# Carried states laid out as diagonal blocks by GpSimd and multiplied by 8 full-size products behind x's transposes; x's high part on VectorE

## The reference

```python
gammas = 1.0 - 2.0 ** (-5.0 - jnp.arange(h))
q = (x @ W_q.T).reshape(b, t, h, dh)          # k and v the same
decay = jnp.where(diff >= 0, gammas[:, None, None] ** pow_, 0.0)
attn = jnp.einsum('bihd,bjhd->bhij', q, k) * decay[None] / scale
y = jnp.einsum('bhij,bjhd->bihd', attn, v)
mean = y.mean(axis=(1, 3), keepdims=True); var = y.var(axis=(1, 3), keepdims=True)
yn = ((y - mean) / jnp.sqrt(var + EPS)).reshape(b, t, dm) * gn_weight + gn_bias
x = x + yn @ W_o.T
...
shared = silu(xf @ sw1 + sb1) * (xf @ sw3 + sb3) @ sw2 + sb2
h = gelu(jnp.einsum('enc,ech->enh', xs, w1) + b1[:, None, :], approximate=False)
y = jnp.einsum('enh,ehc->enc', h, w2) + b2[:, None, :]
```

## Time and profile before

| | |
|---|---|
| median of 3 runs | 443.07 us (442.89 to 443.53) |
| profiled execution: its own time, its span | 443.2 us, 441.4 us |
| granted TensorE clock, mean | 0.996 |
| PE, PEld busy | 433.1 us, 391.6 us |
| DVE, ACT, POOL busy | 292.7, 216.3, 95.6 us |
| phase 1 | from the span's start to about 200 us |

### The profile page before, as it was taken

The page is one execution under the profiler, slowest core; times in us unless marked ns, Lnnn a source line. Parts: engine busy times, 40 slices in busy tenths (PEclk is TensorE's granted clock), DMA queues, the critical chain, the costliest instruction groups (busy, mean ns, idle before and its releaser), DMA issues.

```text
span 441.4 us, 14549 instructions
## 1 busy us (share of the span) xinstructions
PE 433.1 (98%) x6318; PEld 391.6 (89%) x6318; DVE 292.7 (66%) x685; ACT 216.3 (49%) x416; POOL 95.6 (22%) x73
## 2 busy tenths in 40 slices
PE   6999999999999999999999999999999999999997
PEld 4999999999999999998989988899988999888995
DVE  6777778766886878967556654757538575475433
ACT  3456656546754477445255443472524823346430
POOL 1103223522254213640621101211004020040000
PEclk8999999999999999999999999999999999999999
DMA  7443332232321131226230005000133001120011
GB/s 260 146 148 99 99 99 76 75 94 80 126 95 51 51 124 54 91 79 222 94 115 1 26 25 208 31 0 0 48 122 116 0 0 48 48 95 0 1 48 48
DMA packets 15382, 34.64 MB, mean 78 GB/s; under 512 B 2368, under 2 KB 2656, under 8 KB 14816
## 3 DMA queue, kind: packets, MB, share of 16 engines
q1 hardware_dynamic: 14896, 33.05, 22.0%
q10 hardware_dynamic: 432, 0.79, 0.5%
HBM read 25.44 MB, written 8.40 MB: 77 GB/s over the span
## 4 chain that ended last, share of the span: by engine, by line
PE 91%; ACT 3%; DVE 3%; DMA 1%; issue 1%; POOL 0%; DVEq 0%; ACTq 0%
PE bank L358 50%; PE bank L367 13%; PE bank L368 7%; PE bank L437 5%; PE bank L480 4%; PE bank L467 3%; PE bank L451 2%; PE bank L563 2%; PE bank L416 1%; PE bank L377 1%; ACT kexp L681 1%; ACT vexp L681 1%; DMA xin<-xa 1%; PE bank L498 1%; DVE pm L873 1%
## 5 line engine op out<-in xcount | busy, mean ns | idle before, releaser
L778 ACT ACTIVATE xres<-bank,r1b 128x256 f32<-128x256 f32 x64 | 26.8, 470 | 54.9 <-PE bank L368 53.6
L358 PE MATMUL bank<-x2hi,sw_hi 128*128 128x512 f32 x128 | 51.3, 400 | 0.0
L763 ACT ACTIVATE sil<-bank,s1b 128x512 f32<-128x512 f32 x32 | 22.0, 688 | 58.4 <-PE bank L358 58.3
L358 PE MATMUL bank<-x2lo,sw_hi 128*128 128x512 f32 x128 | 50.4, 394 | 0.0
L358 PE MATMUL bank<-x2hi,sw_lo 128*128 128x512 f32 x128 | 50.3, 393 | 0.0
L696 ACT ACTIVATE keo<-kT,msk 128x512 f32<-128x512 f32 x32 | 21.4, 715 | 51.9 <-DVE kT L862 51.9
L367 PE MATMUL bank<-sw_both,ghi 128*128 128x512 f32 x128 | 46.5, 396 | 0.0
L367 PE MATMUL bank<-w_both,ehi 128*128 128x512 f32 x128 | 46.4, 397 | 0.0
L1045 DVE SCALAR_TENSOR_TENSOR gf<-bank,s3b,sil 128x512 f32<-128x512 f32 x32 | 23.9, 748 | 32.4 <-PE bank L358 32.4
L873 DVE TENSOR_TENSOR pm<-bank,msk 128x512 f32<-128x512 f32 x64 | 39.5, 679 | 2.3 <-PE bank L437 2.2
L358 PE MATMUL bank<-xhi,wqkv_hi 128*128 128x256 f32 x128 | 38.6, 302 | 0.9 <-DVE xlo L857 0.7
(11 more groups left out here) (119 smaller groups left out, 1133.7 us busy)
## 6 DMA issues: line engine op xcount, KB each, us to landing
xin<-xa SPq DMA_DIRECT2D x16, 256.0 KB, 3.3
w_raw<-w SPq DMA_DIRECT2D x16, 256.0 KB, 3.3
xres<-xs SPq DMA_DIRECT2D x16, 256.0 KB, 3.4
x_scratch<-xres SPq DMA_DIRECT2D x16, 256.0 KB, 3.4
xl<-x_scratch SPq DMA_DIRECT2D x8, 512.0 KB, 5.2
xr<-x_scratch SPq DMA_DIRECT2D x4, 1024.0 KB, 4.8
out<-xr SPq DMA_DIRECT2D x7, 512.0 KB, 2.6
sw_raw<-sw SPq DMA_DIRECT2D x6, 256.0 KB, 3.7
```

The lines of the kernel that those rows point to most:

```text
L358: mm = nc.tensor.matmul(o, w[c][l], x[c][r], start=first and c == 0 and j == 0, stop=last and c == n - 1 and j == 2)
L763: nc.scalar.activation(sil[i % 2][:], h1_bank[i % 2][:], ACT.Silu, bias=s1b[:, m:m + 1]).then_inc(sil_ready, 1)
L778: ge = nc.scalar.activation(hf[q % 2][:, m, :], e_bank[q % 4][:, m * 2 * P:(m + 1) * 2 * P], ACT.Gelu, bias=r1b[:, e, m:m + 1])
```

## The change

The 32 small products of a step's from_state become 8 full-size ones (6 where s is 0): a new buffer `wide` (128 partitions x 2 groups x 4 chunks x 128 columns) holds the four 32x32 states of a group and chunk as blocks on the diagonal of a 128x128 matrix, zero elsewhere. GpSimd clears it once and copies the blocks in with four copies of 32 partitions in every step (widen_state), before its other work of the step. from_state stands between transpose_x(h+2) and scores(h+1). high_x, apart from its first two calls, is DVE's; ACT takes high_y behind copy_k and copy_v; DVE takes low_y and y_sums last. The loads of slot_bias stand behind phase 1's last stores, and its buffer has another place in SBUF.

```diff
-            def from_state(h, opens):
-
-                pe.wait_ge(s_ready, h + 1)
...
-                        for p in range(PAIRS):
-                            at = slice(32 * p, 32 * p + 32)
-                            mm = nc.tensor.matmul(y_bank[at, o:o + CH], state[h % 2][at, g, c, :], qT[h % 2][at, g, c * CH:(c + 1) * CH],
-                                                  start=(opens and c == first and g == 0), stop=not opens, skip_group_check=True)
...
+            def from_state(h):
+
+                pe.wait_ge(wide_ready, h + 1)
+                for c in range(0 if h % NSUP else 1, CPS):
                     for g in range(GROUPS):
                         o = g * SUPER + c * CH
...
+                        mm = nc.tensor.matmul(y_bank[:, o:o + CH], wide[:, g, c, :], qT[h % 2][:, g, c * CH:(c + 1) * CH],
+                                              start=False, stop=True, skip_group_check=True)
+                mm.then_inc(y_done, 1)
...
                 if h + 1 < PARTS:
-                    from_scores(h, True)
-                    from_state(h, False)
+                    from_scores(h)
                 else:
-                    from_state(h, True)
+                    pe.wait_ge(s_ready, h + 1)
...
-                    from_scores(h, False)
+                    from_scores(h)
+                    from_state(h)
...
                     project_v(h + 1)
                     if h + 2 < PARTS:
                         transpose_x(h + 2)
+                    from_state(h)
                     scores(h + 1)
...
-                high_y(h)
                 if h + 1 < PARTS:
                     copy_k(h + 1)
                     copy_v(h + 1)
-                if h + 2 < PARTS:
-                    high_x(h + 2)
+                high_y(h)
...
+            def high_x(h):
+
+                dve.wait_ge(t_done, h + 1)
+                nc.vector.tensor_copy(xhi[:].rearrange("p c t -> p (c t)"), b_bank[:]).then_inc(xhi_ready, 1)
...
-                low_y(h)
-                y_sums(h)
                 if h + 3 < PARTS:
                     ln_apply(h + 3)
-                else:
-                    ln2_apply(0, h + 3 - PARTS)
                 if b and s >= 2:
                     for j in range(2 * (s - 2), 2 * (s - 2) + 2):
                         residual(b - 1, j, p_bank[j])
+                if h + 3 >= PARTS:
+                    ln2_apply(0, h + 3 - PARTS)
                 if h + 2 < PARTS:
+                    high_x(h + 2)
                     low_x(h + 2)
+                low_y(h)
+                y_sums(h)
...
+            def widen_state(h):
+                settled(h)
+                pool.wait_ge(s_ready, h + 1)
+                if h:
+                    pool.wait_ge(y_done, h)
+                chunks = slice(0 if h % NSUP else 1, CPS)
+                for p in range(PAIRS):
+                    at = slice(32 * p, 32 * p + 32)
+                    cp = nc.gpsimd.tensor_copy(wide[at, :, chunks, at], state[h % 2][at, :, chunks, :])
+                cp.then_inc(wide_ready, 1)
+                pool.wait_ge(wide_ready, h + 1)
+
             def step(h):
                 b, s = h // NSUP, h % NSUP
+                widen_state(h)
```

More of the change, by code:

```diff
@@ L133, in moe_retention @@
             state = [sb_1(f"state{i}", [P, GROUPS, CPS + 1, 32]) for i in range(2)]
+            wide = sb_1("wide", [P, GROUPS, CPS, P])
             qT = [sb_1(f"qT{i}", [P, GROUPS, SUPER]) for i in range(2)]
@@ L165, in moe_retention @@
         elo = [sb(f"elo{i}", [P, MR, 2 * P], F32R) for i in range(4)]
+        slot_bias = sb("slot_bias", [P, NE, D])
         def const(name):
@@ L193, in moe_retention @@
             sem(n) for n in ("sc_done", "pm_ready", "y_done", "yhi_ready", "ylo_ready", "y_stats"))
-        s_done, s_first, s_ready, s_carried = (sem(n) for n in ("s_done", "s_first", "s_ready", "s_carried"))
+        s_done, s_first, s_ready, s_carried, wide_cleared, wide_ready = (
+            sem(n) for n in ("s_done", "s_first", "s_ready", "s_carried", "wide_cleared", "wide_ready"))
         gn_aggr, gn_mean, gn_dev, gn_sq, gn_e, gn_var, gn_ve, gn_rstd, gn_a, gn_ma, gn_ready = (
@@ L337, in _ @@
                 store_x1(last, j)
+            sp.wait_ge(bias_stored, 16)
+            sp.wait_ge(o_done, NBATCH * 4)
+            sp.wait_ge(xres_biased, NBATCH * 4)
+            for j in range(4):
+                load_slot_bias(j)
             for j in range(4):
@@ L454, in state_sums, with from_scores @@
                 mm.then_inc(s_done, 1)
-            def from_state(h, opens):
-                pe.wait_ge(s_ready, h + 1)
[L459 to L462, removed]
+            def from_state(h):
+                pe.wait_ge(wide_ready, h + 1)
+                for c in range(0 if h % NSUP else 1, CPS):
                     for g in range(GROUPS):
                         o = g * SUPER + c * CH
-                        for p in range(PAIRS):
-                            at = slice(32 * p, 32 * p + 32)
-                            mm = nc.tensor.matmul(y_bank[at, o:o + CH], state[h % 2][at, g, c, :], qT[h % 2][at, g, c * CH:(c + 1) * CH],
-                                                  start=(opens and c == first and g == 0), stop=not opens, skip_group_check=True)
-                if not opens:
-                    mm.then_inc(y_done, 1)
-            def from_scores(h, opens):
+                        mm = nc.tensor.matmul(y_bank[:, o:o + CH], wide[:, g, c, :], qT[h % 2][:, g, c * CH:(c + 1) * CH],
+                                              start=False, stop=True, skip_group_check=True)
+                mm.then_inc(y_done, 1)
+            def from_scores(h):
                 pe.wait_ge(pm_ready, (h + 1) * PAIRS)
-                if h and opens:
+                if h:
                     pe.wait_ge(y_stats, h)
@@ L479, in from_scores @@
                         for p in range(PAIRS):
[L480 to L484, removed]
+                            nc.tensor.matmul(y_bank[32 * p:32 * p + 32, o:o + CH], vexp[h % 2][:, c, g * PAIRS + p, :],
+                                             pm[p][:, c * GROUPS + g, :], start=(c == 0 and g == 0), stop=False, skip_group_check=True)
             def head_means(b, bank):
@@ L880, in add_state @@
                 dve.wait_ge(s_done, h + 1)
+                if h >= 2:
+                    dve.wait_ge(wide_ready, h - 1)
                 sums = a_bank[:, 0:GROUPS * CPS * 32].rearrange("p (g c e) -> p g c e", g=GROUPS, c=CPS)
@@ L896, in carry_state @@
                 dve.wait_ge(s_ready, h + 1)
+                if h:
+                    dve.wait_ge(wide_ready, h)
                 for g in range(GROUPS):
@@ L1166, in low_ffn, with settled @@
                 nc.gpsimd.tensor_tensor(w.lo[:, at], w.raw[:, at], w.hi[:, at].bitcast(F32), ALU.subtract).then_inc(ffn_lo, 1)
+            def settled(h):
+                b, s = (h - 1) // NSUP, (h - 1) % NSUP
+                if h == 0:
+                    pool.wait_ge(ln_rstd, 3)
+                elif h - 1 in LOW_STEPS:
+                    pool.wait_ge(ffn_lo, LOW_STEPS.index(h - 1) + 1)
+                elif b and s == 1:
+                    pool.wait_ge(xres_biased, b * 4)
+                elif h == 2:
+                    pool.wait_ge(bias_part, 4)
+                else:
+                    pool.wait_ge(ln_rstd, h + 3)
+            def widen_state(h):
+                settled(h)
+                pool.wait_ge(s_ready, h + 1)
+                if h:
+                    pool.wait_ge(y_done, h)
[5 more added lines that the diff above has]
+                pool.wait_ge(wide_ready, h + 1)
             def step(h):
                 b, s = h // NSUP, h % NSUP
+                widen_state(h)
                 if b and s == 0:
@@ L1217, in _ @@
             nc.gpsimd.memset(kexp[:], 0.0).then_inc(kexp_cleared, 1)
-            for h in range(3):
+            ln_power(0)
+            nc.gpsimd.memset(wide[:], 0.0).then_inc(wide_cleared, 1)
+            for h in range(1, 3):
                 ln_power(h)
+            pool.wait_ge(wide_cleared, 1)
             for h in range(PARTS):
```

8 lines of the change are left out of this document (1 added, 7 removed).

## The result

The changed kernel takes 459.35 us (458.65 to 462.12, 6 runs), the kernel before 443.38 in the same runs; the ratio is 1.0364, 95% interval 1.0335 to 1.0392. The profiled execution took 459.01 us with a span of 457.2, 15.8 more than before.

What follows compares the result with a forecast made beforehand. PE was taken to bound the kernel. 443.2 + 12.0 for products + 4.5 for bb_ready - 0.9 for waits won = 458.8 us (6 in 10, own range 456 to 463); whole range 453 to 466.5, 8.5 in 10.

Steps and rivals of the forecast that it cites:

- Products, 12.0 us: PE's from_state in phase 1: full-size products at 0.115 us a record replace small ones, adding 12.0 us.
- bb_ready, 4.5 us: Steps 5, 9 and 13: PE's output_bias waits for POOL's y_bb copy, 1.5 us each, 4.5 in all.
- Waits won, -0.9 us: Phase 1: PE's three waits for xlo and one for xres go, winning 0.9 us.
- what costs nothing: Phase 1 and slot_bias: wide_ready, high_x on DVE, later y_done and late slot_bias loads cost PE nothing.
- DVE's busy time should rise by 9 us: Sign in the changed kernel's profile: DVE is busy for 9 us more.
- slot_bias, nothing: After phase 1: the four loads can come over 10 us later unseen, at no cost.
- Rivals 2 and 4: from_state: loads hidden, 446.6 us, 1 in 10; or pace of 0.041 us, faster than before, 441.1 us, 0.5 in 10.
- rival 1: POOL's copies cost 0.85 us each, waits for bb_ready 9.9 us, total 464.2 us; chance 1.5 in 10.
- Rival 3: Steps 5, 9 and 13: no wait for bb_ready, total 454.3 us; chance 1 in 10.

Runs made afterwards that it cites:

- experiment 3: Changed kernel with from_state's full-size products on 32 of each chunk's 64 columns: 462.57 us, ratio 1.0458.
- experiment 9: Changed kernel with each full-size product of wide cut into two diagonal halves, 64 rows by 64 columns, side by side: 451.76 us, ratio 1.0239.
- experiment 1: Changed kernel with POOL's copy into y_bb ahead of the copies into wide in steps where s is 1: 453.74 us, ratio 1.025.
- experiment 7: Kernel before with high_x alone moved from ACT to DVE, directly ahead of low_x: 441.89 us, ratio 0.998.
- experiment 5: Changed kernel without wide, its copies and waits; small products in the new place, slot_bias as before: 445.14 us, ratio 1.007.
- experiment 10: Changed kernel with the edits of experiment 1 and experiment 9 together: 446.52 us, ratio 1.0094.
- experiment 4: Kernel before with only the four slot_bias loads moved behind phase 1's last stores, POOL waiting for them at its addition: 443.67 us, ratio 1.0027.
- experiment 6: Changed kernel with POOL's addition of slot_bias cut to 2 elements of each partition, loads and waits kept: 457.9 us.
- experiment 8: Changed kernel run once more, unaltered, beside the other experiments' kernels: 459.02 us, ratio 1.0381 to the kernel before.
- experiments 2: Changed kernel with copies into wide kept, but from_state multiplying the small state blocks in its new place: 454.89 us, ratio 1.0295.

## Why the prediction was right

The forecast was 458.8 us, the changed kernel takes 459.35. By its terms, with what was measured:

- **Products, 12.0 us.** The mechanism is right: experiment 3 shows that the load and not its 64 columns sets the pace, experiment 9 with the earlier trace rows that the load's width does. The size was too high. I took 0.115 us a record, between 0.11 (the means' loads) and 0.121 (the scores), and it is 0.108, slightly under my lower row. 11 x 0.70 + 4 x 0.49 + 0.90 (step 15, 1.93 for 1.03) = 10.6 us. The scores were no bound for it: their 0.121 is for four loads beside one another. The estimate from the Trainium skill (TensorE: Matmul & The Clock Gate, LDWEIGHTS), 10.1 for this term, was nearer than my sum; 0.107 against 0.108 is as good as exact here.
- **bb_ready, 4.5 us.** Right in its place, its steps and its cause (experiment 1); 5.6 us measured, 1.87 each for 1.5. Of the 0.4, the masks began 1.39 us into step 5 where I had 1.2, the four copies took 1.71 for 1.6 and y_bb 0.47 for 0.40.
- **Waits won, -0.9 us.** Right: gone from the trace, and high_x alone wins 0.7 (experiment 7). But the step "what costs nothing" left out DVE's line ahead of the masks in the s = 1 steps. It is hidden behind the wait for y_bb in the changed kernel, and shows once that is gone: 1.1 us of waits in experiment 5, 2.3 in experiment 10. The sign "DVE's busy time should rise by 9 us" was wrong too, 18.5 measured.
- **slot_bias, nothing.** This term was put at nothing and is 0.9. I compared when the sum is ready with when it is needed, and that was right, but not what runs beside the addition: DVE's low_gate stands for 5 us, and 0.9 us of it reaches PE (experiments 4 and 6). The Trainium skill (SBUF — State Buffer, SBUF: two separate sides) says that a GpSimd instruction which reads SBUF and a VectorE instruction with two SBUF inputs lock each other out for a whole instruction. The trace agrees: low_gate has two such inputs, gf and ghi, POOL's addition reads xr and slot_bias, and the 5.01 us of low_gate end 0.55 us behind the addition's 4.64, where it takes 0.68 alone.

Together: 10.6 + 5.6 - 0.9 + 0.9 = 16.2 us, less the 0.4 by which step 0 began earlier, is the span's 15.8; the 0.4 is the clock, and beside experiment 8 the change costs 16.4. My 15.6 came this close by luck in part: a term 1.4 too large stood beside two that were 1.1 and 0.9 too small. Of the 4.1 us by which experiment 10 ends above the kernel before, the waits for the masks are 2.3, that for gf 0.7, that for xlo in step 14 0.7 and the products 0.8 (0.04 to 0.05 in each of 16 steps), less the 0.9 won; the remaining 0.5 is not accounted for.

Rivals 2 and 4 fell with the 0.108 us of a record, rival 1 with the copies' 397 ns. Rival 3 was what experiment 1 builds: the forecast for it was 454.3, and 453.74 was measured.

## What to carry to other kernels

Small float32 products that lie side by side in the array, with few columns each, are not made cheaper by joining them in a block-diagonal matrix: the full-width load costs 0.108 us with 64 columns to multiply and 0.107 with 32, four loads of 32 columns side by side 0.064. Where an engine gets a new piece of work at the head of a step, look at everything that stands behind it in the same step, and who waits for that; a small copy behind a late one cost half as much as the whole change in products. And ask of a moved instruction not only when its result is needed but what runs beside it; a mean far above the median, as low_gate's, is where to look. Before taking the difference of two traces, look at the granted clock ahead of the first step.

## What was not expected of the hardware

With fewer columns on PE the kernel was slower. In the profiled execution of experiment 3 the granted clock fell to the lower of TensorE's two levels, 1.2 for 2.4 GHz, for parts of steps 5, 6 and 9; all four executions had a mean clock of 0.984 to 0.989. Busy time and clock by stretch (us, PE, PEld, DVE, ACT, POOL; PEclk, DMA share, GB/s):

```profile
62.76:73.80 11.04, 11.04 (x257) 10.66 (x253) 9.03 (x28) 5.79 (x12) 2.72 (x6) 1.00 0.32 96
73.80:87.68 13.88, 13.49 (x260) 12.87 (x257) 11.23 (x30) 6.25 (x14) 8.71 (x10) 0.87 0.21 60
87.68:95.00 7.32, 7.32 (x164) 7.03 (x161) 5.53 (x15) 1.34 (x2) 2.93 (x6) 0.77 0.29 86
95.00:103.06 8.06, 8.06 (x119) 7.95 (x118) 4.84 (x12) 4.57 (x10) 3.09 (x2) 1.00 0.09 26
```

and in its chain, the pieces there against 0.83 and 3.07 us elsewhere:

```profile
87.75 1.44 PE bank L455 x64
89.19 3.87 PE bank L362 x24
```

Steps 6 and 9 take 15.4 and 15.5 us there for 14.0 and 13.9; in step 5 the slower stretch only shortens the wait for y_bb, 0.4 for 1.9. What PE did before each fall differs. In step 9 it had waited for y_bb from 132.9 to 134.9 us, and the clock is at 0.50 from 135.4 on. In step 5 the clock is at 0.51 from 73.9 on, ahead of that step's wait and behind steps in which PE had waited for nothing, and at the end of step 5 it fell 7 us behind the wait. Ahead of those two PE had not stood idle; the last it had done were the products with half the columns and the scores.

With all 64 columns the stretches are rarer. In the profiled execution of experiment 6 there are two, and both begin right behind a wait for y_bb (130.6 to 132.6, then 0.50 from 132.8 on; 185.2 to 187.1, then 0.50 from 187.4 on); steps 9 and 13 take 15.5 us for 13.9. Two of the twelve executions of the changed kernel have a clock of 0.993 and take 462.12 and 462.43 us, some 3.3 more than the rest. No execution of experiments 1, 7 and 10, which have no wait for y_bb, was below 0.999. That the wait carries a second, occasional price fits this, but no run shows it alone: experiment 4, without such a wait, has one execution at 0.995, and experiments 2 and 9, with it, have executions at 0.991 to 0.996 of which no trace tells where the clock fell. Neither my sum nor the median holds such a price.
